# Depthwise 13x13 convolution: patch halves loaded from ScalarE's and GpSimd's queues at one moment, none from SyncE's

## What is computed

```python
    def _L1_conv_ref(x, w_large, w_small, ...):          # w_large 13x13, w_small 3x3, one filter for each channel
        out = _bn(_dwconv(x, w_large, kl // 2), g_l, b_l, m_l, v_l) + _bn(_dwconv(x, w_small, ks // 2), g_s, b_s, m_s, v_s) + _bn(x, g_i, b_i, m_i, v_i)
        return out
    ...
    x = x + _L1_conv_ref(_gn(x), ...)
```

## Time and profile before

| | |
|---|---|
| median of 3 runs | 2936.91 us (2936.56 to 2945.85) |
| the profiled execution | 2936.08 us, span 2934.1 us |
| TensorE (PE) | 2590.5 us busy, 88% of the span |
| VectorE (DVE) | 2522.6 us, 86% |
| ScalarE (ACT) | 1476.5 us, 50% |
| GpSimd (POOL) | 74.9 us, 3% |
| DMA | 546.95 MB, mean 186 GB/s |
| granted clock of TensorE, mean | 0.977 |

### The profile page before, as it was taken

How to read it: one execution, slowest core, us unless ns; L and a number is a source line. 1 busy time by engine, 2 the same in 40 slices (tenths; PEclk the granted TensorE clock), 3 DMA queues, 4 the chain that set the end, 5 groups by cost and what they waited for, 6 DMA issues and landing times. The chain is left out here.

```text
span 2934.1 us, 50706 instructions
## 1 busy us (share of the span) xinstructions
PE 2590.5 (88%) x17273; PEld 1861.0 (63%) x17273; DVE 2522.6 (86%) x3512; ACT 1476.5 (50%) x1921; POOL 74.9 (3%) x144
## 2 busy tenths in 40 slices
PE   0049999999999999999995999993799999999998
PEld 0026666666666666666663656663688888888887
DVE  7968999999999999999997889894877778877784
ACT  0043445554554555554321676773655566555663
POOL 0010000000000000000000000000000000000000
PEclk9999999999999999999997999996899999999999
DMA  8965112322322331321002899996999999999996
GB/s 331 416 206 160 49 42 91 105 79 88 101 84 79 104 94 68 110 90 59 6 12 107 282 341 346 348 342 159 243 266 272 282 279 275 276 266 264 275 273 186
DMA packets 349112, 546.95 MB, mean 186 GB/s; under 512 B 143392, under 2 KB 254752, under 8 KB 345888
## 3 DMA queue, kind: packets, MB, share of 16 engines
q1 hardware_dynamic: 317504, 436.49, 48.0%
q10 hardware_dynamic: 31456, 108.48, 12.6%
HBM read 364.47 MB, written 180.44 MB: 186 GB/s over the span
## 5 line engine op out<-in xcount | busy, mean ns | idle before, releaser
L781 PE MATMUL qk_qb<-qk_xhi,whi 128*128 128x384 f16 x2592 | 846.1, 326 | 21.0 <-DVE qk_xlo L677 14.3
L781 PE MATMUL qk_qb<-qk_xlo,whi 128*128 128x384 f16 x2592 | 846.2, 326 | 0.0
L781 PE MATMUL qk_qb<-qk_xhi,wlo 128*128 128x384 f16 x2592 | 846.0, 326 | 0.0
L698 DVE SCALAR_TENSOR_TENSOR qk_dw<-qk_pool,qk_wd,qk_dw 128x768 f32<-128x768 f32 (+2 forms) x864 | 837.9, 1010 | 0.9 <-ACT qk_dw L550 0.8
L685 DVE TENSOR_REDUCE qk_pool<-qk_qb 128x192 f32<-128x768 f32 x432 | 412.0, 954 | 67.1 <-PE qk_qb L781 50.7
L1633 PE MATMUL cv_cb<-cv_hi,cv_toep 128*128 128x288 f16 x1536 | 350.8, 289 | 74.8 <-DMA cv_toep<-toeplitz_scratch 41.7
L781 PEld LDWEIGHTS qk_qb<-qk_xhi,whi 128*128 128x128 f16 x2592 | 254.0, 98 | 184.2 <-DVE qk_xlo L677 17.7
L781 PEld LDWEIGHTS qk_qb<-qk_xhi,wlo 128*128 128x128 f16 x2592 | 253.9, 98 | 168.2 <-issue 1.0
L1497 ACT ACTIVATE cv_res<-cv_cb,cv_cst 128x288 f32<-128x288 f32 x384 | 186.5, 501 | 343.4 <-PE cv_cb L1639 278.9
L781 PEld LDWEIGHTS qk_qb<-qk_xlo,whi 128*128 128x128 f16 x2592 | 253.8, 98 | 162.8 <-issue 0.7
L1639 PE MATMUL cv_cb<-cv_hi_next,cv_toep 128*128 128x288 f16 x1536 | 350.0, 289 | 0.0
(11 more groups left out here) (164 smaller groups left out, 3504.2 us busy)
## 6 DMA issues: line engine op xcount, KB each, us to landing
cv_toep<-toeplitz_scratch SPq DMA_DIRECT2D x384, 256.0 KB, 8.3
patch_scratch<-pr_turned SPq DMA_DIRECT2D x75, 832.0 KB, 9.7
st_x<-in_x SPq DMA_DIRECT2D x24, 2304.0 KB, 17.1
qk_xf<-in_x SPq DMA_DIRECT2D x72, 768.0 KB, 4.2
pr_xb<-in_x SPq DMA_DIRECT2D x24, 2304.0 KB, 9.9
out<-cv_rows ACTq DMA_DIRECT2D x72, 768.0 KB, 7.4
cv_raw<-patch_scratch SPq DMA_DIRECT2D x25, 1300.0 KB, 16.6
cv_raw<-patch_scratch ACTq DMA_DIRECT2D x23, 1300.0 KB, 11.1
```

Of the source, the lines that this page charges most:

```text
L698: V.scalar_tensor_tensor(acc, pool[:, o, r + y:r + y + n, x:x + PW], wd[:, o, k:k + 1], acc, ALU.mult, ALU.add).then_inc(taps_done, 1)
L781: ins = nc.tensor.matmul(qbank[s % NQB][:, h, 0:2 * W], w[:, b, o * P:(o + 1) * P], x[:, par, j // 2, b, at_row:at_row + 2 * W], start=n = ...
```

## The change

Each half gets its own semaphores (`lower_in`, `upper_in`). All lower halves but group 0's go to ScalarE's queue, where the upper ones were. All upper halves go to GpSimd's queue. GpSimd waits for `edge_done`, as before, and for the first channel of the group (`conv_done`), which is what stands ahead of ScalarE's load too. SyncE has no patch load left in the stage; it keeps the lower half of group 0.

```diff
     def first_load(sp):
-        for h in range(2):
-            load_half(sp, 0, 0, h)
+        load_lower(sp, 0, 0)
 
     def masks(gp):
 
         G = nc.gpsimd
+        load_upper(gp, 0, 0)
         G.memset(colsel[:, :], 1.0).then_inc(masked, 1)
...
                 for c in range(GRP):
-                    if at(g, 0) and c == 2:
-                        start.load_half(sp, 1, 1, 0)
-                    if c == NTOEP + 1 and (inner or g + 2 < NG):
-                        address(sp, (g + 2) * (TI * GRP * TJ))
-                        sp.wait_ge(edge_done, g * NPC + NPC)
-                        start.load_half(sp, g + 2, par, 0)
                     if inner or g < NG:
                         load_taps(g, c)
...
         def _(gp):
+            start.load_upper(gp, 1, 1)
             nc.gpsimd.memset(late[:, :, 1, :], 0.0).then_inc(late_zero, 1)
+
+            def step(g, par, inner=False):
+                if inner or g + 2 < NG:
+                    address(gp, (g + 2) * (TI * GRP * TJ))
+                    gp.wait_ge(edge_done, g * NPC + NPC)
+                    gp.wait_ge(conv_done, g * GRP + 1)
+                    start.load_upper(gp, g + 2, par)
+
+            run(gp, step, tail=NG - 2)
...
-            start.load_half(act, 1, 1, 1)
+            start.load_lower(act, 1, 1)
...
-                        start.load_half(act, g + 2, par, 1)
+                        start.load_lower(act, g + 2, par)
...
                 if q == 0:
-                    dve.wait_ge(raw_in[par], (g // 2) * 32 + 32 if isinstance(g, int) else (g - par) * 16 + 32)
+                    for half in (lower_in[par], upper_in[par]):
+                        dve.wait_ge(half, (g // 2) * 16 + 16 if isinstance(g, int) else (g - par) * 8 + 16)
```

More of the change, by code:

```diff
@@ L1297, in depthwise_start, with half_rows, load_lower, load_upper @@
     rowsel = sb("rowsel", [P, TW])
-    raw_in = [ctx.enter_context(nc.semaphore(f"cv_raw_in{i}")) for i in range(2)]
+    lower_in = [ctx.enter_context(nc.semaphore(f"cv_lower_in{i}")) for i in range(2)]
+    upper_in = [ctx.enter_context(nc.semaphore(f"cv_upper_in{i}")) for i in range(2)]
     masked = ctx.enter_context(nc.semaphore("cv_masked"))
     PITCH = NG * TI * GRP * TJ
-    def load_half(eng, g, par, h):
+    def half_rows(g, h):
         v = patch_dram[h * HALF_ROWS:h * HALF_ROWS + 1, bass.ds(g, 1), :, :].rearrange("p a i n -> p (a i n)")
-        eng.dma_start(raw[h * HP:(h + 1) * HP, par].rearrange("p i c j -> p (i c j)"),
-                      bass.AP(v.tensor, v.offset, [[TH * PITCH, TW], [PITCH, HALF_ROWS], [1, TI * GRP * TJ]])).then_inc(raw_in[par], 16)
+        return bass.AP(v.tensor, v.offset, [[TH * PITCH, TW], [PITCH, HALF_ROWS], [1, TI * GRP * TJ]])
+    def load_lower(eng, g, par):
+        eng.dma_start(raw[0:HP, par].rearrange("p i c j -> p (i c j)"), half_rows(g, 0)).then_inc(lower_in[par], 16)
+    def load_upper(eng, g, par):
+        eng.dma_start(raw[HP:P, par].rearrange("p i c j -> p (i c j)"), half_rows(g, 1)).then_inc(upper_in[par], 16)
     def first_load(sp):
-        for h in range(2):
-            load_half(sp, 0, 0, h)
+        load_lower(sp, 0, 0)
     def masks(gp):
         G = nc.gpsimd
+        load_upper(gp, 0, 0)
         G.memset(colsel[:, :], 1.0).then_inc(masked, 1)
@@ L1330, in depthwise_start @@
     start.raw, start.toep, start.side, start.colsel, start.rowsel = raw, toep, side, colsel, rowsel
-    start.raw_in, start.masked, start.NTOEP = raw_in, masked, NTOEP
-    start.load_half, start.first_load, start.masks = load_half, first_load, masks
+    start.lower_in, start.upper_in, start.masked, start.NTOEP = lower_in, upper_in, masked, NTOEP
+    start.load_lower, start.load_upper, start.first_load, start.masks = load_lower, load_upper, first_load, masks
     return start
@@ L1354, in stage_depthwise @@
         raw, toep, side, colsel, rowsel = start.raw, start.toep, start.side, start.colsel, start.rowsel
-        raw_in, masked = start.raw_in, start.masked
+        lower_in, upper_in, masked = start.lower_in, start.upper_in, start.masked
         norm = sb("norm", [P, 2, CPP, TJ, TI])
```

## The result

The changed kernel takes 2958.43 us (median of 20 runs, 2939.39 to 2968.29) against 2936.9 (20 runs, 2931.02 to 2952.88): ratio 1.0066, 95% interval 1.005 to 1.0082. It is slower by 21.5 us, where 17 us less was forecast. The profiled execution is the slowest of the 20, 2968.29 us with a span of 2966.5; the fastest had a span of 2937.5.

What follows compares the result with a forecast made beforehand. The prediction took TensorE's waits for late `toep`, behind a patch half, to bound the kernel: 2936.1 - 37.0 (old waits) + 19 (new waits) + 1 (start of the stage) = 2919 us, range 2898 to 2958.

Steps and rivals of the forecast that it cites:

- What bounds the kernel: Depthwise stage: TensorE waits 37.0 us for late `toep`, 1.85 us per group, at channel 9 behind SyncE's lower half.
- the start: Start of the stage: first matmul 2.6 us later, a 2.17 us wait gone, GpSimd's issue about 0.6 more; sum +1 us.
- The place of the new wait: In each group, channel 8's `toep` is next in need and comes through about 0.8 us behind both halves.
- the first rival: Halves stay in line; channel 8's wait grows to 3.7 us, +44 us, 2980; chance of slower, milder forms included, 0.24.
- I take the middle, 0.6 us: Channel 8's wait in the group studied, between 0.4 us and 0.8 us; 0.35 was added for the mean.
- 276 GB/s: Rate with both halves of group 2 under way, 2080 to 2084; at it both halves need 9.6 us.
- the sum: Whole kernel: 2936.1 - 37.0 + 19 + 1 = 2919 us, the 19 being 0.95 us in each of 20 groups.
- the 4.9 us of the working: Part of the upper half's 11.3 us from issue to landing: start, stores and `late` ahead of its own bytes.
- the 249 from which the first rival decides: Below 249 GB/s both halves need over 10.7 us and channel 8's `toep` comes more than 1.5 us late.
- the second one: Second of two `toep` waits at the stage's start: belongs to group 2 and stays; the 2.17 us wait goes.
- GpSimd's queue: GpSimd's transfers start late or set up slowly, perhaps colliding with VectorE's copies: nothing to 6.4 us; chance 0.04.
- The second rival, no change: The wait moves from channel 9 to channel 8 at its old size; 245 to 262 GB/s, 2928 to 2945; chance 0.20.

Runs made afterwards that it cites:

- spaced kernel: Changed kernel, but GpSimd asks for the upper half behind channel 8 of the group instead of channel 0: 2883.09 us, ratio 0.9819.
- the run with the unread matmuls: Changed kernel plus 9 matmuls into a spare PSUM bank, result unread, ahead of the wait for channel 8's matrices in each group: 2936.35 us, ratio 1.0004.

## Why the prediction was wrong

**What bounds the kernel** was right. `toep` of one channel in each group is late by a patch half, and this costs more than its wait: with the halves apart the kernel is at 2883 us, 53 us below the kernel before, of which 37.0 are waits of TensorE in the steady state. Of the other 16, ten are the six clock falls of the kernel before, which the spaced kernel doesn't have, and the two waits of the start are 4.7, of which a start later by 3.4 us (2067.31 against 2063.89) takes most back. Some 4 us stay unplaced.

**The place of the new wait** was right: channel 8, behind both halves, as the first rival had it.

**The step that failed** is "I take the middle, 0.6 us", the size of that wait. It rested on both halves having landed after 14.5 us, from 276 GB/s, or 14.9. Measured were 16.2, then 1 us to the matrices: a wait of 1.97 us in this group and 2.37 in the mean, where the sum had 0.95. All 20 came to 47.3 us, where the sum had 19. The 276 GB/s came from one stretch of 4 us; the three windows above give 262, 246 and 209. Taking out the 4.9 us of the working, 2.66 MB in 11.3 us are 236 GB/s, 14% over the 207 of one half, and under the 249 from which the first rival decides. That rival was the right one, in a milder form: waits of +10 us, not +44.

The rule of the Trainium skill ("SBUF — State Buffer", "Can I just issue two DMAs to hit both halves?") says +6%. The trace agrees as closely as it can tell. A half that runs alone lands 10.4 to 10.7 us after its issue (medians of the spaced variant), of which its own bytes at 207 GB/s are 6.4; that leaves 4.0 to 4.3 us ahead of them, where my working had 4.9. Two halves together are through after 16.4 us. By an estimate from these, 2.66 MB took 11.5 to 12.4 us: 215 to 231 GB/s, a gain of 4 to 12%. And two queues instead of one gave only some 0.3 us. I should have weighed the rule more heavily against a row of 4 us.

**A term was missing:** the clock, which the sum put at nothing. The waits became only 10.3 us longer in all (47.3 against 37.0), and the start gave +3.7 and, with no wait left for `toep` there (the prediction let the second one stay), took back 4.7. These alone are 9.3 us, about 0.3%. But behind every wait the clock now falls: 16 falls more than before in the steady state and two fewer at the start, 14 in all, 24 us at 1.7 each. Together this is 33 us, against 32.4 between the profiled spans. Held against the forecast, the waits missed by 28 us, the falls by 24, and the start by 2 the other way: 50, where the profiled execution is 49 us above 2919.

The profiled execution is the slowest of the 20, so these shares are those of a bad case; at the median the change costs 21.5 us. The spread of the runs fits: at a mean clock of 0.977 the changed kernel's span was 2937.5 us, at 0.968 2966.5. What shows the clock as a cause is the run with the unread matmuls: the transfers are as late, 19 falls are gone, and the profiled span is 31 us shorter. What decides whether a wait brings a fall is not shown.

**The other rivals.** GpSimd's queue is not to blame: 493 ns for an issue, landings of 9.7 and 10.7 us in the spaced variant, like SyncE's and ScalarE's (10.3 to 12.3 us with SyncE's half at channel 15). That it meets VectorE's copies was not seen in any time. The second rival, no change, was worked out slightly wrong: by the prediction's own terms 245 to 262 GB/s give 2926 to 2940 us, not 2928 to 2945. The range, 2898 to 2958, was missed by 0.4 us, at its upper end; a slower kernel had a chance of 0.28.

## What to carry to other kernels

When a large transfer delays a stream of small ones that are just in time, look for the distance between the large ones before you look for another queue: here moving one of two loads by six places in its own queue gave 1.9%, and moving both to other queues at one moment cost 0.7%. Ask how far ahead the ring of the small ones reaches (a ring of 8: channel 8's matrices are asked for behind channel 0 and needed 7 channels later, here 14.3 us, from 2289.1 to 2303.4), and keep what the large ones take between two needs well under it. And when a wait of TensorE grows, put a price on the clock behind it as well: here waits that grew by 0.5 us each (10 us in all) came with 14 more clock falls, 24 us, in the slowest run.

## What I had not expected of the hardware

- Two transfers of 1.33 MB into partitions 0 to 63 and 64 to 127, issued 0.3 us apart on ScalarE's and GpSimd's queues, were through only some 0.3 us sooner than on one queue, of some 16 (medians of 20 groups).
- The granted clock went to half for 3.4 us behind waits of 1.93 to 3.52 us in all 20 groups of the changed kernel, whereas in the kernel before waits of 1.97 and 2.02 us passed without one. At the start of the stage, the variant with SyncE's half at channel 15 passed one of 3.5 us without. So the length of the wait alone doesn't decide it.
- Nine unread matmuls ahead of each of 20 waits took 19 clock falls away and were worth 22 us in a kernel of 2958.
